# Eleven GpSimd powers moved behind the low halves of the next step

## The reference

```python
x = x + tanh(g_xattn) * xattn(_layernorm(x), ctx, ctx, mask, Wq..bo)   # 16 heads of 8 channels, rope on q and k
x = x + tanh(g_ffn)   * ffn(_layernorm(x), W1, b1, W2, b2, Wr, br)     # 8 experts, each row goes to one

def _layernorm(x):  m, v = mean(x), var(x);  return (x - m) / sqrt(v + 1e-5)
```

## Time and profile before

| | us |
|---|---|
| timed runs, median (lowest to highest) | 280.02 (279.95 to 280.26) |
| the profiled execution | 283.1 |
| its span, first to last instruction | 281.2 |
| busy in the span: PE, DVE, ACT, POOL | 234.1, 191.5, 167.2, 182.7 |
| eight powers of the first norm (line 491) | 8.3 (1032 ns each) |
| five powers of the second norm (line 499) | 7.1 (1425 ns each) |
| granted TensorE clock, mean | 0.983 of full |

### The profile page before, as it was taken

How to read it: one execution, slowest core, us unless ns; L and a number is a source line. 1 busy time by engine, 2 the same in 40 slices (tenths; PEclk the granted TensorE clock), 3 DMA queues, 4 the chain that set the end, 5 groups by cost and what they waited for, 6 DMA issues and landing times.

```text
span 281.2 us, 10499 instructions
## 1 busy us (share of the span) xinstructions
PE 234.1 (83%) x3529; PEld 203.5 (72%) x3529; DVE 191.5 (68%) x639; ACT 167.2 (59%) x484; POOL 182.7 (65%) x222
## 2 busy tenths in 40 slices
PE   1357898989799898787897899588889999999992
PEld 1235777878578777666776787477778899999992
DVE  5545777888789979998778977868568434434430
ACT  1235678878577787666886777626473434444440
POOL 7374755757646889746988687660747727747645
PEclk9999999999799999999999999979999999999998
DMA  7711355618445464512525122133204423321100
GB/s 217 229 37 28 86 156 148 175 30 213 104 100 145 115 157 115 147 27 40 145 53 148 36 48 47 30 82 100 65 34 139 122 73 91 96 80 41 51 20 20
DMA packets 58535, 26.63 MB, mean 95 GB/s; under 512 B 38608, under 2 KB 53989, under 8 KB 58484
## 3 DMA queue, kind: packets, MB, share of 16 engines
q1 hardware_dynamic: 55204, 20.15, 29.3%
q0 software_dynamic: 2272, 4.46, 4.7%
q10 hardware_dynamic: 1008, 1.35, 1.6%
HBM read 16.70 MB, written 5.51 MB: 79 GB/s over the span
## 4 chain that ended last, share of the span: by engine, by line
PE 48%; DVE 16%; POOL 11%; issue 8%; DMA 6%; ACT 5%; SPq 3%; POOLq 1%; DVEq 0%; ACTq 0%
PE ps L760 13%; PE ps L803 5%; DMA kbd<-kT 4%; PE ps L741 3%; PE ps L818 3%; PE ps L743 3%; PE ps L742 3%; DVE mx L1252 3%; SPq L407 3%; POOL rot L548 2%; POOL rot L542 2%; PE ps L793 2%; PE ps L779 2%; POOL rot_s L544 2%; POOL stk L527 2%
## 5 line engine op out<-in xcount | busy, mean ns | idle before, releaser
L565 POOL DMA_INDIRECT out<-fin,got x39 | 38.1, 978 | 23.8 <-issue 13.0
L1252 DVE TENSOR_REDUCE mx<-ps 128x16 f16<-128x1024 f32 x32 | 39.1, 1222 | 16.5 <-PE ps L818 16.3
L513 POOL DMA_INDIRECT rows<-x_all,dest_i x32 | 33.3, 1041 | 20.3 <-DVE x_all L1080 9.7
L760 PE MATMUL ps<-w_f,hT 128*128 x312 | 44.6, 286 | 0.0
L803 PE MATMUL ps<-vx,pr 128*64 128x32 f32 x1024 | 37.4, 228 | 4.4 <-DVE on L1180 2.4
L803 PEld LDWEIGHTS ps<-vx,pr 128*64 128x64 f32 x1024 | 33.8, 142 | 8.2 <-issue 2.9
L760 PEld LDWEIGHTS ps<-w_f,hT 128*128 128x128 f32 x312 | 37.8, 191 | 0.8
L601 ACT ACTIVATE pr<-ps 128x1024 f32<-128x1024 f32 x32 | 32.8, 1024 | 9.2 <-PE ps L845 8.7
L542 POOL TENSOR_TENSOR rot<-qk,cf 128x256 f32<-128x256 f32 x32 | 23.5, 735 | 22.4 <-ACT qk L623 15.8
L1310 DVE SCALAR_TENSOR_TENSOR fin<-ps,got 128x128 f32<-128x128 f32 x39 | 13.7, 351 | 35.0 <-PE ps L760 35.0
L527 POOL TENSOR_TENSOR stk<-rot,stk 128x256 f16<-128x256 f32 x32 | 21.8, 682 | 23.9 <-DVE stk L1264 23.9
(11 more groups left out here) (161 smaller groups left out, 586.2 us busy)
## 6 DMA issues: line engine op xcount, KB each, us to landing
kbd<-kT SPq DMA_DIRECT2D x128, 32.0 KB
got<-rows SPq DMA_DIRECT2D x39, 72.0 KB, 1.9
w_f<-in_W_rows SPq DMA_DIRECT2D x8, 256.0 KB, 3.0
w_r<-in_W_last_row SPq DMA_DIRECT2D x8, 256.0 KB, 3.9
w_f<-in_L_ffn_W SPq DMA_DIRECT2D x8, 256.0 KB, 5.3
x_all<-in_x SPq DMA_DIRECT2D x3, 512.0 KB, 4.8
xt_all<-in_x_t SPq DMA_DIRECT2D x3, 512.0 KB, 4.3
ct_all<-in_ctx SPq DMA_DIRECT2D x3, 512.0 KB, 4.5
```

Of the source, the lines that this page charges most:

```text
L513: pool.indirect_dma_start(out=rows, out_offset=bass.IndirectOffsetOnAxis(ap=dest_i[:, t:t + 1], axis=0), in_=x_all[:, t, :], in_offset=Non ...
L565: pool.indirect_dma_start(out=out_d, out_offset=bass.IndirectOffsetOnAxis(ap=got_i[:, u % GOT, R_ID:R_ID + 1], axis=0), in_=fin[:, u % FRI ...
L760: mm = pe.matmul(o, hT[:, par, c, :], w2_f[:, bass.ds(e, 1), c, :].rearrange("p o n -> p (o n)"), start=False, stop=(c == FC - 1))
L1252: dve.tensor_reduce(mx[:, t % 2, 0:H], ps_s[:, :].rearrange("p (h k) -> p h k", k=S), AX.X, ALU.max).then_inc(mx_done, 1)
```

## The change

```diff
-        RSTD_AT = {1: 1, 3: 2, 7: 3, 11: 4, 15: 5, 19: 6, 23: 7}
+        RSTD_AT = {2: 1, 4: 2, 8: 3, 13: 4, 16: 5, 21: 6, 24: 7}
...
                     pool.tensor_tensor(win[:, :, 16:24], f, win[:, :, 8:16], ALU.subtract).then_inc(lo_done, 1)
-                if i == max(GROUP_AT):
+                if i in RSTD_AT:
+                    rstd_of(RSTD_AT[i])
+                if i - 1 in GROUP_AT and i <= T:
+                    rstd2_of(GROUP_AT[i - 1])
+                if i in GROUP_AT and i >= T:
                     rstd2_of(GROUP_AT[i])
                 for _ in range(SCATTER_AT.get(i, 0)):
                     scatter()
...
-                if i in RSTD_AT:
-                    rstd_of(RSTD_AT[i])
-                if i in GROUP_AT and i < max(GROUP_AT):
-                    rstd2_of(GROUP_AT[i])
```

## The result

The changed kernel takes 286.88 us (median of 286.21, 285.49, 287.55 and 290.04); the ratio to before is 1.018, 95% interval 1.0137 to 1.0224, so +5.0 us (3.8 to 6.3). The forecast was a sum of +4.75 us, 284.8 as the time, with a range of 282.1 to 286.9: direction and size of the change are right. The median itself is 6.9 us above that of before, 2.1 above the forecast, and only just inside the range: the three times of before that the forecast started from lie within 0.3 us, while 57 later ones go from 277.67 to 284.88. The terms of the sum are less right than the sum, and the reason is the main lesson of this case.

A forecast was written before the change was run, and what follows sets the result against it. No engine was taken to bound the whole span: a ring of engines closes each attention step, TensorE bounds the expert tiles. Terms -1.5 + 0 + 2.1 + 2.8 + 1.35 = +4.75 us on 280.02 gave 284.8, range 282.1 to 286.9.

The forecast's parts named there:

- part 1: Steps 11 to 12: low half starts 1.4 us earlier, TensorE's wait shrinks; -1.5 us, bounds 1.08 and 3.0.
- part 2: Steps 1 to 8: powers 1, 2 and 3 move to steps 2, 4 and 8, about no effect; 0.
- part 3: Steps 15 to 27: powers behind the low halves lie on GpSimd's own ring and delay it; +2.1 us.
- part 4: Step 32: power waits for variance, scatters and row load come 4.2 us late, 1.4 spare; z +2.8 us.
- clock behind the stall: Behind TensorE's 3.4 us without work, its clock falls; +1.35 us, between 0 and 1.6.
- The rule on shared ports: Step 12: a power would push VectorE's line 1195 back by up to 0.8 us; the sum assumed it doesn't.
- Step 19: Group power there delays scatter and rope by 0.6 us; taken as hidden, up to 0.4 if not.
- The clock does not fall in the new wait: Rival at the new TensorE wait: no clock fall there, 283.4 us; chance 0.17.
- Faster: Rival at VectorE's z: first rows are in time, 280.6 or 278.5 us; chance 0.05 below, 0.03 near no change.
- A further loss: Rival in the attention steps: VectorE or TensorE loses more, 285.6 or 286.0 us; chance of either 0.14.
- first form: A power holds up VectorE's two-input SBUF operations for its whole length; at step 12 up to 0.8 us, 285.6.
- second form: TensorE waits about 0.9 us longer for low halves behind two late ropes, another clock fall; about +1.2, 286.0.

The follow-up runs named there:

- e5: The kernel before, unchanged, profiled a second time; the execution took 280.8 us, span 278.9.
- e8: The kernel before with only group 2's power moved from step 25 to behind step 26's low halves; 280.72 us against 281.78, ratio 0.9945.
- e9: The kernel before with only the power moves of steps 12 and 26; 280.9 us against 281.8, ratio 0.9943.
- e11: The kernel before with only the powers of steps 1, 3 and 7 moved behind the low halves of 2, 4 and 8; 281.44 us, ratio 0.9984.
- e3: The kernel before with only step 11's two powers moved, behind the low halves of steps 12 and 13; 281.1 us against 280.64, ratio 1.005.
- e12: The kernel before with group 3's power between the second and third of step 32's four scatters; 283.06 us against 281.8, ratio 1.0051.
- e2: The kernel before with only group 3's power of step 32 moved in front of the four scatters; 286.27 us, ratio 1.0219.
- e10: e9 with added, never-read products in three TensorE waits of steps 31 and 32; 279.15 us, ratio to before 0.9943.
- e6: The changed kernel, unchanged, profiled and timed again beside the kernel before; 286.76 us, ratio to before 1.0169.
- e7: The changed kernel with 14 added, never-read products in TensorE's wait at the start of step 34; 284.92 us, ratio to before 1.0121.

## Why the prediction was right, and where not

| term | forecast | between the two profiles | from all profiles, falls set apart |
|---|---|---|---|
| part 1, step 12 | -1.5 | -2.06 | -0.31 (15.77 - 16.08) |
| part 2, steps 1 to 8 | 0 | +0.25 | +0.6 (66.2 - 65.6), not shown by the times |
| part 3, steps 15 to 27 | +2.1 | +0.68 | +0.7 (97.54 - 96.87) to 1.4 (97.54 - 96.1) |
| part 4, stall at z | +2.8 | +2.8 | +3.74 (23.99 - 20.25) |
| clock behind the stall | +1.35 | +1.4 | +1.5 to 2.0 |

The last column sums to 6.2 to 7.4. Against it stand the falls that before has of its own: at step 12 in 2 of 6 profiles with its order there, 1.5 to 1.75 us each (17.60 and 17.83 against 16.08), and at step 32 in 5 of 7 (before, e5, e8, e9, e11, not e3 and e12), 0.9 to 1.2 us, once 1.9. That is some 0.5 + 0.9 = 1.4 us in the mean, which leaves +4.8 to 6.0; measured were 5.0 and, with 1.0169 of 281.8, 4.8. The falls are not all of the scatter: of the 57 later runs of before, the 12 with a mean granted clock of 0.995 or more have a median of 279.75 us, the others 281.98, but the 12 alone go from 277.67 to 283.39. Late loads are a further part (the d stretches of the table); the rest was not looked for.

- **Part 1** failed in size. The step that failed is "what is late next is VectorE ... the gain is at least 1.08": the max's wait for TensorE at 76.34 was a product of the fall, and without it the end moves by 0.31. The lower bound was read from the stretch behind the fall itself. Where the fall comes, the gain is 1.8 to 2.1, inside the stated bounds.
- **The rule on shared ports.** Line 1195 took 0.68 us beside a power in after, and 0.69 in the earlier trace rows: a power of a few elements holds up nothing, as the sum had it. The rope passes do: lines 990 and 1018 took 1.09 and 1.15 us beside them, 0.36 and 0.35 where they began ahead of them, and line 1195 itself took 2.08 us beside them in e2. That is what the Trainium skill, page "SBUF — State Buffer", section "Who interferes with whom", says of a VectorE instruction with two inputs in SBUF and a GpSimd one that reads SBUF; the traces agree for passes over 128 x 256, not for powers. What decides in close cases stays open: line 1018 of step 20 begins 0.12 to 0.28 us ahead of two passes in every profile and still takes 1.62 to 1.78 us, and line 990 of step 12 of after begins within a pass and takes 0.38.
- **Part 2** was taken as hidden. Tile 4's low halves come 0.6 to 0.8 us later behind the power of step 4; by tile 10 some 0.6 us is left in the profiles. Not settled by the times.
- **Part 3**: step 16 (+0.88 forecast) measured +0.86. Step 24 (+0.63) measured +0.4 in sum: 0.78 from tile 23 to 24, less 0.39 from tile 19 to 23, where the power is gone. Step 26 (+0.61) measured +0.62, and step 28 gave back 1.06: there the sentence that "the rows around 98.59 show GpSimd with no idle time but those 0.61" was true of step 16 and not of step 28, where GpSimd had waited 1.98 us for VectorE. Step 19 was hidden against the profile of before (11.87 against 12.02) and against e8, e9 and e10 (11.95 to 12.11), and is not against e3, e5 and e12 (11.24, so +0.63, above the stated 0.4). The difference is again line 990, 1.09 us in before and 0.36 in e5:

```profile
111.25 1.09 DVE L990 TENSOR_TENSOR logit<-x_all 128x56 f32<-128x56 f32 x1
```
```profile
107.81 1.56 POOL L513 DMA_INDIRECT rows<-x_all,dest_i  x1 [0.18 <-POOL stk L527]
109.11 0.36 DVE L990 TENSOR_TENSOR logit<-x_all 128x56 f32<-128x56 f32 x1
```

In e5 the scatter took 1.56 us in place of 1.06, the rope came later, line 990 began 0.3 us ahead of it and was not held, and the step ended 0.7 us earlier: here a slower scatter makes a faster step. e3 and e12 show the same. In all three the scatter began 0.05 us behind VectorE's line 1199; in before it began 0.15 us ahead of it.
- **Part 4** was right in kind at each point: the new wait of GpSimd for line 984, the scatters behind it, the late load (11.47 - 7.31 = 4.16, forecast 4.2), the wait at z, TensorE idle over 3 us, the clock at half behind it. The slack was wrong: 1.4 us were read from an execution whose TensorE had just lost about 1.1 us to a fall; without it nothing is spare, and the stall costs 3.74.
- The two errors come from one source and have opposite signs: the falls in the profile of before made the gain of part 1 too large by 1.2 and the loss of part 4 too small by 0.9. The sum came out right for that reason as much as for its working.
- "I take the difference as it is" (3.1 us between profile and median of before) hid this. A profile 3.1 us above the median is a sign of something in that one execution, and its windows showed what: two stretches at half clock, which cost 1.75 and 1.1 us by the table.
- **Rivals.** "The clock does not fall in the new wait": it fell in all three profiles with the stall and no filling (after, e2, e6), and e7 shows what that costs. "Faster" had no support: nothing made the load's lateness harmless. "A further loss": its first form did not come, as line 1195 beside the power of step 12 shows. Of the second form, after has one more fall, at step 20, behind a wait of TensorE of 1.72 us; it cost 0.1 us (22.49 from tile 19 to 23 against 22.41 in e6, which had no fall there). But that wait is for VectorE's max, not for low halves, and e2 and e10, which have the order of before there, fell at the same place.

## What to carry to other kernels

Before a wait or a slack is read from a profile, look at the granted clock of that stretch and at how far the profiled execution is from the timed median: where the clock is at half, the waits behind it and the slack ahead of the next load belong to that execution, and a second profile of the same kernel is the cheapest experiment there is. Work that is put in front of what another queue waits for costs its own wait too: one power moved ahead of four scatters cost as much as the whole change. A long engine wait that can't be removed can be filled with idle products on TensorE, if they end before it does.

## What was not expected of the hardware

- TensorE's clock falls behind the same waits in some executions and not in others: at step 12 (wait 1.67 to 1.90 us) in 2 of 6 profiles, at step 32 (waits of 0.91 and 0.97 us one after the other) in 7 of the 13 without added products there. In after it fell at 36 us behind a wait of 0.89 us and did not fall at 186 us behind one of 1.26.
- What a fall costs depends on who is late: 1.5 to 2.0 us behind the stall, 0.9 to 1.2 at step 32 (1.9 in e11, where it lasted longer), and 0.1 at step 20 of after.
- GpSimd's power takes 1.01 to 1.09 us for four elements per partition (once 1.17), 1.33 for six and 1.51 to 1.60 for seven, as long as two rope passes over 256 elements.
- A two-input instruction of VectorE over 56 elements takes 0.18 to 0.36 us where nothing holds it and 1.09 to 1.78 where two rope passes do; one over 512 elements took 2.04 to 2.08 in place of 0.68. A GpSimd instruction of 0.67 us took 0.82 to 1.05 beside VectorE's line 1195.
